# Cross-attention scores: stacked 128-row products replaced by 32-row tiles

## What is computed

```python
q = proj(hs, Wq, bq, S); k = proj(at, Wk, bk, T); v = proj(at, Wv, bv, T)    # 16 heads of 32
scores = jnp.einsum('bhsd,bhtd->bhst', q, k) / math.sqrt(32)
scores = jnp.clip(scores, -50.0, 50.0)
scores = jnp.where(attend, scores, -10000.0)
scores = jnp.clip(scores, -50.0, 50.0)
probs = jax.nn.softmax(scores, axis=-1)
ctx = jnp.einsum('bhst,bhtd->bhsd', probs, v)
```

## Time and profile before

| | |
|---|---|
| time, median of 3 runs | 826.15 us (825.44 to 826.71) |
| the profiled execution's own time | 824.42 us |
| its span | 822.7 us |
| TensorE matmul busy | 747.9 us, 91% |
| VectorE busy | 602.8 us, 73% |
| ScalarE busy | 405.5 us, 49% |
| GpSimd busy | 12.8 us, 2% |
| mean granted TensorE clock | 0.964 |

### The profile page before, as it was taken

How to read it: one execution, slowest core, us unless ns; L and a number is a source line. 1 busy time by engine, 2 the same in 40 slices (tenths; PEclk the granted TensorE clock), 3 DMA queues, 4 the chain that set the end, 5 groups by cost and what they waited for, 6 DMA issues and landing times.

```text
span 822.7 us, 15196 instructions
## 1 busy us (share of the span) xinstructions
PE 747.9 (91%) x5776; PEld 476.5 (58%) x5776; DVE 602.8 (73%) x955; ACT 405.5 (49%) x536; POOL 12.8 (2%) x35
## 2 busy tenths in 40 slices
PE   4995999999999999847599995789999999999997
PEld 2642555554555455415377772567777777777774
DVE  5474888888888786443588885468888888888885
ACT  4363566657666656501366663234444444444442
POOL 1200000000000000000000000000000000000000
PEclk9998999999999999987799999689999999999999
DMA  7469050605051323022014400077676677777770
GB/s 284 119 210 298 3 120 36 154 0 153 1 153 30 76 54 101 27 114 91 1 78 153 153 26 0 4 246 230 232 247 228 227 237 244 231 229 234 246 230 28
DMA packets 37031, 113.72 MB, mean 138 GB/s; under 512 B 8528, under 2 KB 18176, under 8 KB 34432
## 3 DMA queue, kind: packets, MB, share of 16 engines
q1 hardware_dynamic: 36448, 112.64, 43.5%
q0 software_dynamic: 256, 0.52, 0.3%
q10 hardware_dynamic: 288, 0.02, 0.0%
HBM read 94.73 MB, written 0.57 MB: 116 GB/s over the span
## 4 chain that ended last, share of the span: by engine, by line
PE 71%; issue 16%; DVE 4%; DMA 3%; SPq 3%; ACT 1%; POOL 0%; DVEq 0%; POOLq 0%; ACTq 0%
PE pS L974 32%; PE pP L974 23%; PE pD L974 8%; PE pO L974 8%; DMA arena<-in_ctxT 2%; SPq L279 1%; DMA arena<-in_wkT 1%; PE pS L986 1%; SPq L229 1%; ACT arena L493 0%; DVE bn L648 0%; DMA arena<-w_scratch 0%; DVE arena L681 0%; ACT xT L425 0%; SPq L251 0%
## 5 line engine op out<-in xcount | busy, mean ns | idle before, releaser
L974 PE MATMUL pS<-arena 128*128 128x256 f16 (+2 forms) x2706 | 335.8, 279 | 7.9 <-DVE arena L768 3.7
L974 PEld LDWEIGHTS pS<-arena 128*128 128x128 f16 (+1 forms) x2706 | 270.8, 102 | 81.5 <-issue 13.4
L974 PE MATMUL pP<-arena 128*128 128x512 f16 x984 | 240.1, 385 | 19.6 <-DVE arena L662 10.6
L974 PEld LDWEIGHTS pP<-arena 128*128 128x128 f16 x984 | 92.8, 99 | 146.4 <-issue 36.8
L493 ACT ACTIVATE arena<-pS,mblk 128x1024 f32<-128x1024 f32 x128 | 146.9, 1201 | 4.7 <-PE pS L974 4.4
L887 DVE SCALAR_TENSOR_TENSOR arena<-arena 128x1536 f16<-128x1536 f32 x72 | 126.1, 1752 | 2.4 <-ACT arena L590 2.4
L723 DVE TENSOR_SCALAR arena<-arena 128x1024 f32<-128x1024 f32 x128 | 88.2, 693 | 47.6 <-ACT arena L493 47.2
L607 ACT ACTIVATE arena<-pS 128x256 f32<-128x256 f32 x72 | 27.6, 383 | 164.3 <-PE pS L974 164.3
L590 ACT ACTIVATE arena<-arena 128x1536 f16<-128x1536 f32 x72 | 106.3, 1477 | 0.0
L974 PE MATMUL pO<-arena 128*32 128x256 f32 (+4 forms) x1216 | 85.8, 365 | 3.7 <-DVE arena L847 3.1
L974 PE MATMUL pD<-arena 128*128 128x512 f16 x312 | 81.2, 379 | 4.8 <-DVE arena L949 3.3
(11 more groups left out here) (166 smaller groups left out, 461.0 us busy)
## 6 DMA issues: line engine op xcount, KB each, us to landing
arena<-in_units SPq DMA_DIRECT2D x72, 768.0 KB, 4.8
arena<-arena SPq DMA_DIRECT2D x112, 128.0 KB, 2.4
arena<-w_scratch SPq DMA_DIRECT2D x144, 64.0 KB, 2.6
arena<-in_ctxT SPq DMA_DIRECT2D x8, 1024.0 KB, 6.1
mw_in<-in_mla_in SPq DMA_DIRECT2D x8, 1024.0 KB, 6.7
mw_out<-in_mla_out SPq DMA_DIRECT2D x8, 512.0 KB, 3.3
arena<-arena SPq DMA_DIRECT2D x32, 64.0 KB, 2.0
arena<-in_wkT SPq DMA_DIRECT2D x1, 1024.0 KB, 5.0
```

Source lines behind the costliest of these rows:

```text
L974: return pe.matmul(o, lhsT, rhs, start=start, stop=stop, **kw)
```

## The change

The scores are computed on natural K and q, without stacking. A step's scores of four heads are three rounds of four matmuls. Matmul j of a round takes rows 32j to 32j+31 of both operands and writes bank j of `pS`; the rounds are kh·qh, kl·qh and kh·ql, accumulated. The product kl·ql is left out. `pS` is shared out anew: each head has a bank, and the two steps of a pair take its lower and upper 256 columns. `kh` and `kl` become double-buffered. The scores of a pair are done together: one wait for both exponentials of the pair before, one signal at the end. All stacking transfers, their buffers and their waits are gone. The 32-row tiles are only in the scores of the cross-attention; the latent attention is the same in both kernels.

```diff
         def step_scores(st):
-            return pS[:, 2 * (st % 2):2 * (st % 2) + 2, :].rearrange("p b (h q) -> p (b h) q", h=2)
+            return pS[:, :, T * (st % 2):T * (st % 2) + T]
...
-        kh = take(HC * CB, f16).rearrange("p (g t) -> p g t", g=HC)
-        kl = take(HC * CB, f16).rearrange("p (g t) -> p g t", g=HC)
+        kh, kl = (take(2 * HC * CB, f16).rearrange("p (b g t) -> p b g t", b=2, g=HC) for _ in range(2))
...
-            stack_k0(0, s["k0_stacked"])
-            sp.wait_ge(s["q_lo"], 1)
-            stack_q(sp, 2, 4, s["q_rest"])
-            stack_k0(2, s["k0_rest"])
...
-                if stack:
-
-                    sp.wait_ge(s["exp_done"], STEPS * b + 1)
-                    sp.nop()
-                    load_mask(b + 1, 1 - p)
-                    stack_k(b + 1, 1 - p)
+                sp.wait_ge(s["exp_done"], STEPS * b + 1)
+                sp.nop()
+                load_mask(b + 1, 1 - p)
...
-            pool.wait_ge(s["q_lo"], 1)
-            stack_q(pool, 0, 2, s["q_stacked"])
...
-                        act.wait_ge(s["scores_done"], STEPS * b + st + 1)
+                        act.wait_ge(s["scores_done"], PAIRS_X * b + i + 1)
...
-            def split_k(b, n):
-
-                if n == 0 and not (isinstance(b, int) and b == 0):
-                    if isinstance(b, int) and b == 1:
-                        dve.wait_ge(s["k0_stacked"], 16 * STACK_DMAS)
-                        dve.wait_ge(s["k0_rest"], 16 * STACK_DMAS)
-                    else:
-                        dve.wait_ge(s["k_stacked"], 16 * STACK_DMAS * (b - 1))
+            def split_k(b, p, n):
+
...
-            def scores(b, p, st):
-
-                g, tile = st // CT, st % CT
-                if not (isinstance(b, int) and b == 0 and st < 2):
-                    pe.wait_ge(s["exp_done"], STEPS * b + st - 1)
-                for j in range(4):
-                    last = mm(step_scores(st)[:, j, :], k_st[:, p, j, g, 128 * tile:128 * tile + 128],
-                              q_st[:, j, g, :], True, True)
+            def scores(b, p, i):
+
+                first = isinstance(b, int) and b == 0
+                if first and i % 2 == 0:
+                    pe.wait_ge(s["k_lo"], i // 2 + 1)
+                if not first and i == 0:
+                    pe.wait_ge(s["k_lo"], 4 * (b + 1))
+                if not (first and i == 0):
+                    pe.wait_ge(s["exp_done"], STEPS * b + 2 * i)
+                for st in (2 * i, 2 * i + 1):
+                    g, tile = st // CT, st % CT
+                    for k, (w, x) in enumerate(((kh, qh), (kl, qh), (kh, ql))):
+                        for j in range(4):
+                            r = slice(32 * j, 32 * j + 32)
+                            last = mm(step_scores(st)[:, j, :], w[r, p, g, 128 * tile:128 * tile + 128], x[r, g, :],
+                                      k == 0, k == 2)
                 last.then_inc(s["scores_done"], 1)
```

More of the change, by code:

```diff
@@ L122, in build @@
         wqT = v_sb[:, 1]
-        q_st = take(XH * T, f16).rearrange("p (j g q) -> p j g q", j=4, g=HC)
         probs = take(CT * 4 * T).rearrange("p (b j q) -> p b j q", b=CT, j=4)
@@ L126, in build @@
         psums = (psum4, xT[:, :, :])
[L127 to L131, removed]
+        wk32, wv32 = (take(HC * HID).rearrange("p (c n) -> p c n", c=HC) for _ in range(2))
         qh, ql = (work[:, i, :].bitcast(f16).rearrange("p (g q) -> p g q", g=HC) for i in range(2))
@@ L203, in build @@
             aux_in var_ready rstd_ready xn_ready tr_done xT_ready
-            const_ready zc_ready prep_ready wk_hi wk_lo q_mm q_f q_hi q_lo q_stacked q_rest
-            ctx_hi ctx_lo proj_done proj_evac k_hi k_lo k0_stacked k0_rest k_stacked
+            const_ready zc_ready prep_ready wk_hi wk_lo q_mm q_f q_hi q_lo
+            ctx_hi ctx_lo proj_done proj_evac k_hi k_lo
             scores_done exp_done clip_done pv_done sum_done dsum_done
@@ L221, in build @@
         wb_in = [sem(f"wb_in{i}") for i in range(RING)]
[L223 to L229, removed]
         block = ctx.enter_context(nc.Block())
@@ L272, in _ @@
             load_ctx(1, 1)
[L274 to L278, removed]
-                        sp.dma_start(k_st[32 * part:32 * part + 32, 0, j, g:g + 2], src[32 * j:32 * j + 32, g:g + 2, :])\
-                          .then_inc(done, 16)
             sp.wait_ge(s["prep_ready"], 1)
             load_mask(0, 0)
-            stack_k0(0, s["k0_stacked"])
-            sp.wait_ge(s["q_lo"], 1)
-            stack_q(sp, 2, 4, s["q_rest"])
-            stack_k0(2, s["k0_rest"])
             for dst, src in ((lnw[:, :], a["lnw"]), (rs[:, :], a["rs"].broadcast_to([128, 1])), (o2n_c[:, :], a["o2n_c"]),
@@ L297, in _, with x_block @@
                 load_mla_out(m, m)
-            def x_block(b, p, stack=True, load=True):
+            def x_block(b, p, load=True):
                 if load:
@@ L693, in _ @@
             norm(x_sb, xn, 1).then_inc(s["xn_ready"], 1)
-            split_k(0, 0)
-            split_k(0, 1)
+            split_k(0, 0, 0)
+            split_k(0, 0, 1)
             for c in range(HC):
@@ L699, in _ @@
                    .then_inc(s["wk_lo"], 1)
-            split_k(0, 2)
+            split_k(0, 0, 2)
             dve.wait_ge(s["q_f"], 1)
@@ L707, in _ @@
             last.then_inc(s["q_lo"], 1)
-            split_k(0, 3)
+            split_k(0, 0, 3)
             for c in range(HC):
@@ L717, in x_block @@
                     if proj and 1 <= i <= HC:
-                        split_k(b + 1, i - 1)
+                        split_k(b + 1, 1 - p, i - 1)
                     g, tile = i // 2, 2 * (i % 2)
@@ L1070, in x_block @@
                 first = isinstance(b, int) and b == 0
-                if first:
-                    pe.wait_ge(s["k0_stacked"], 16 * STACK_DMAS)
-                else:
-                    pe.wait_ge(s["k_stacked"], 16 * STACK_DMAS * b)
                 for i in range(PAIRS_X):
-                    if first and i == HC:
-                        pe.wait_ge(s["k0_rest"], 16 * STACK_DMAS)
-                    scores(b, p, 2 * i)
-                    scores(b, p, 2 * i + 1)
+                    scores(b, p, i)
                     if i:
@@ L1092, in x_block @@
                         project(b + 1, 1 - p, i)
-            pe.wait_ge(s["q_stacked"], 8 * 16)
-            pe.wait_ge(s["q_rest"], 8 * 16)
+            pe.wait_ge(s["q_lo"], 1)
             x_block(0, 0)
```

10 lines of the change are left out of this document (2 added, 8 removed).

## The result

The changed kernel takes 817.62 us (median of four, 816.58 to 818.87), the kernel before 826.27 beside it (825.44 to 826.71). The ratio is 0.9897, with a 95% interval of 0.9877 to 0.9917. It is faster by 1.0%, and inside the predicted range of 804 to 820; the gain is 8.6 us where 14.0 were forecast. The profiled executions, 818.56 us and 824.42 before, lie 5.9 us apart.

The account below looks back on a forecast made before the run. TensorE was taken to bound the kernel, busy all 40 of 40 us in the steady part. Gains of 10.6 and 6.2 less 2.8 make 14.0 us, so 810.4 profiled and 812.2 us as median; range 804 to 820.

Parts of the forecast that it names:

- Standstill, 10.6 us: Block 0, cross-attention: an earlier context load removes TensorE's 9.07 us wait and 1.5 us of slow clock behind it.
- Scores, 0.11 us per pair: Cross-attention scores: a pair costs 0.85 us against 0.96, saving 6.2 us over 56 pairs.
- the 0.67 + 0.09 of the sum: Scores of a pair: six rounds of four matmuls take 0.67 us, one change of tile form 0.09.
- The rival of matmuls limited at 69 ns: Scores: 24 matmuls would take 1.66 us instead of 0.67, the kernel 875; chance 0.12, shared with row groups two by two.
- a sign of slow rounds: Score groups on TensorE: idle time put down to "issue" inside a group would show the forecast wrong; no size given.
- Last block, +2.8: Last block, without projection: TensorE and ScalarE wait on each other, pairs take 3.29 us for 2.84, 2.8 us lost.
- the cover: Blocks with projection: weighing and projection hide the single wait per pair for both exponentials, so it costs nothing.
- VectorE needs its 33.4 us of then 39.1: Steady part of the cross-attention: VectorE's busy time still fits in the shortened stretch.
- early loads that hurt the start: Start: early loads delay the v weights by 7.6 us, 3.1 past their slack, giving 815; chance 0.04.
- a dearer change of form: Scores: the tile form change for 32 rows costs one more 0.09 us per pair, 5.8 us, giving 818; chance 0.13.
- its own 7 us: Scores, best case: rows to columns free and rounds of 0.107 us, 0.12 less per pair; given as reaching 804.

Follow-up runs that it names:

- The kernel with the loads late: Changed kernel with SyncE waiting behind the mask load until four exponentials are done, so the context load is late as before: 827.72 us, ratio 1.0031.
- the experiment on VectorE's order: Changed kernel with VectorE's last context split of a block put ahead of pair 7's two additions: 815.06 us, ratio 0.9869.
- both repaired: Changed kernel with the last context split ahead of pair 7's additions and TensorE's loop over blocks 1 to 4 written out: 812.87 us, ratio 0.9835.
- the longer loop: Kernel before with sixteen one-column zero matmuls ahead of each projection in TensorE's loop over blocks 1 to 4: 838.18 us, one execution.
- head by head: Changed kernel with a pair's 24 score matmuls ordered as six of one row group, then six of the next: 860.96 us, one execution.

## Why the prediction was right, and where it was not

**Standstill, 10.6 us: right**, in mechanism and size. The load was issued at 19.46 for "about 19", and block 0 then runs like the steady part. "What is late next in block 0? Nothing that I find" held too. The kernel with the loads late brings the standstill back, and both with early loads remove it with the old scores.

**Scores, 0.11 us per pair: right.** The pairs of 4.89 and 4.46 were met; over the stage it is 0.107 per pair. Six rounds and the change of form behind them, from rows to columns, whose price was taken from its neighbours, are 0.76 us for the 0.67 + 0.09 of the sum; the change into them is the 0.10 that the projection before them grew by. The rival of matmuls limited at 69 ns is refuted by the same line, with 24 matmuls in 0.76 us, 32 ns each. The Trainium skill's figure of about 62 ns ("TensorE: Matmul & The Clock Gate", Wait — 56ns, not 53.3ns?), cited in the prediction beside that rival, does not bind here either: by it the kernel would have come to about 865, an estimate. The idle time put down to "issue" that the prediction named as a sign of slow rounds did appear, at the start of block 3, but it is the loop's. That the score groups are 0.76 us everywhere else tells the two apart.

**Last block, +2.8: right**, measured at 2.5, with 3.24 us per pair for 3.29.

**What failed is the cover.** The prediction said "In a block with projection this is covered", and of VectorE "VectorE needs its 33.4 us of then 39.1". The second is an average over a stage. At a block's end VectorE has a chain of clip, two additions and a split which ended 0.15 to 0.23 us before it was wanted, and the change took 0.55 from that: 0.32 by TensorE's earlier arrival and 0.23 by the chain's later end, most of it from the exponentials. That is 2.1 us in five blocks, and the experiment on VectorE's order takes it away. The row was there to be read: TensorE's projections at the starts of blocks, and the end of VectorE's split ahead of each.

**What was missing is the loop.** Three times as many score matmuls were priced by their time alone. That they lengthen TensorE's program, and that a loop body may cease to be kept, was no step of the sum; it cost 2.6 us in the first profile and 2.0 in the second. The trace of before had a hint, no instruction packets in the loop's second turn, but no row of it set a price.

With both repaired the cross-attention gains 14.2 us for the 14.0 of the sum. The rest of the distance in the profiled execution, 2.9 us, is the latent stage's clock, which can't be put down to the change.

**That the range held is in part luck.** It reached to 820 for the cases at 815 and 818, early loads that hurt the start and a dearer change of form, and neither came true; the two losses that did come were in no rival. The forecast itself, 812.2, was 5.4 us off. And the lower end of 804 does not follow from its own 7 us, which give 805; nothing rests on it.

**And the reason for the gain was narrower than the change.** The prediction gave 10.6 of 14.0 to the queue, and that was right. What it did not say is that this part needs no new scores. The old scores with a reordered queue are as fast (10.7 us off the cross-attention against 9.4), and the new scores without the early load are 0.3% slower than before.

## What to carry to other kernels

Split the gain of a change into its mechanisms, and ask of each whether a smaller edit has it: here a different order of one DMA queue was worth the whole rewrite. Where a pair of engines gets faster in steps, don't divide busy time by the stage; look at the end of each repeated block for the last operation that the fast engine waits for, and note its slack to a tenth of a microsecond. And count the instructions of a loop as well as their time.

## What the runs showed of the hardware

- Four row groups of 32, with 256 float16 columns each, run wholly beside each other: a round of four took 0.107 to 0.11 us, as long as one full matmul.
- The change of form from full tiles to row tiles costs 0.10 us (the projection before the scores stretches from 2.60 to 2.70), about the 0.09 read for columns; from rows to columns it is some 0.1 too (0.76 less six rounds).
- TensorE started matmuls of a free row group ahead of waiting ones: wholly over runs of three (0.78 us a pair), only partly over runs of six (1.46).
- Sixteen one-column matmuls with their loads took 0.48 us until the next group started, some 30 ns each (the longer loop).
- A TensorE loop with 1280 records of matmuls and loads in its body ran its second turn without instruction packets; with 1792 it refetched, and the jump back cost 2.0 to 2.6 us in six profiles (1.6 in the slowest kernel, head by head).
- In profiles of like code the clock rose to the 2.4 GHz level at either of two times in one stage (within 1.7 us of its start, or 7.5 us behind it), which made the stage 112.9 to 113.1 or 115.5 to 115.9 us long.
